# Two-sample cross-attention kernel on one core: all eight parts of the probability-value product in one visit of the z banks, two-bank evacuations, and new orders on every engine

## What is computed

```python
mu, var = mean(input, axis=(1, 2)), var(input, axis=(1, 2))     # per sample
xn = (input - mu) * rsqrt(var + EPS) * gamma + beta
q  = einsum('oc,ncs->nos', Wq, xn) + bq
kv = einsum('od,nds->nos', Wkv, context) + bkv
att = softmax(einsum('nhqc,nhkc->nhqk', q * scale, k * scale), axis=-1)
y   = einsum('nhqk,nhkc->nhqc', att, v)
out = einsum('co,nos->ncs', Wo, y) + bo
return input + out
```

## Time and profile before

| | |
|---|---|
| median of three runs | 808.37 us |
| profiled execution: its time | 807.66 us |
| profiled execution: span | 805.8 us |
| TensorE busy (matmuls) | 686.3 us, 85% of the span |
| TensorE weight loads | 445.8 us, 55% |
| VectorE busy | 678.0 us, 84% |
| ScalarE busy | 621.6 us, 77% |
| GpSimd busy | 581.7 us, 72% |
| DMA queue of SyncE | 21.6% of what 16 DMA engines could do |
| mean granted clock of TensorE | 0.983 of full |

### The profile page before, as it was taken

How to read it: one execution, slowest core, us unless ns; L and a number is a source line. 1 busy time by engine, 2 the same in 40 slices (tenths; PEclk the granted TensorE clock), 3 DMA queues, 4 the chain that set the end, 5 groups by cost and what they waited for, 6 DMA issues and landing times.

```text
span 805.8 us, 29956 instructions
## 1 busy us (share of the span) xinstructions
PE 686.3 (85%) x11204; PEld 445.8 (55%) x11204; DVE 678.0 (84%) x1124; ACT 621.6 (77%) x2248; POOL 581.7 (72%) x360
## 2 busy tenths in 40 slices
PE   5689988889888888988888988888898888898886
PEld 4355655555655555655555655555565555566453
DVE  1589888898988889898889898888989888989883
ACT  2578778787788878687878788878778778878872
POOL 1478677777777878677877777788777687777763
PEclk9989999999999999999999999999999999999998
DMA  5112222222221222222222221221222122222110
GB/s 111 37 48 68 62 57 67 60 62 62 62 63 51 72 52 64 59 62 53 68 59 58 62 64 52 64 72 51 62 62 62 49 72 53 64 65 52 44 40 15
DMA packets 74814, 47.56 MB, mean 59 GB/s; under 512 B 33748, under 2 KB 74708, under 8 KB 74772
## 3 DMA queue, kind: packets, MB, share of 16 engines
q1 hardware_dynamic: 72848, 46.59, 21.6%
q10 hardware_dynamic: 1924, 0.40, 0.3%
HBM read 25.96 MB, written 4.19 MB: 37 GB/s over the span
## 4 chain that ended last, share of the span: by engine, by line
POOL 41%; issue 37%; PE 9%; DVE 9%; ACT 2%; POOLq 1%; DMA 1%; SPq 1%; ACTq 0%; DVEq 0%
POOL probs L639 32%; POOL xhat L654 6%; DVE probs_t L551 4%; PE z L401 4%; DVE neg_max L538 3%; PE fill L367 3%; POOL rstd L649 3%; ACT probs L483 2%; POOLq L101 1%; PE z L379 1%; DMA wv<-in_L_xattn_Wkv 1%; ACT t L492 1%; DVE recip L544 0%; DVE y L594 0%; SPq L234 0%
## 5 line engine op out<-in xcount | busy, mean ns | idle before, releaser
L639 POOL TENSOR_TENSOR probs<-probs,recip 128x1024 f32<-128x1024 f32 x256 | 483.1, 1893 | 188.5 <-DVE recip L544 184.3
L483 ACT ACTIVATE probs<-fill,neg_max 128x256 f32<-128x256 f32 x1024 | 470.5, 483 | 149.9 <-DVE neg_max L538 149.6
L551 DVE STREAM_TRANSPOSE probs_t<-probs 128x1024 f32<-128x1024 f32 x256 | 313.7, 1225 | 49.7 <-POOL probs L639 46.2
L538 DVE TENSOR_REDUCE neg_max<-fill 128x4 f32<-128x1024 f32 x256 | 306.6, 1198 | 36.3 <-PE fill L367 36.0
L401 PE MATMUL z<-probs_t,ctx_keys 32*64 32x256 f32 x8192 | 260.3, 388 | 69.5 <-DVE probs_t L551 68.3
L367 PE MATMUL fill<-c,t 64*128 64x256 f32 x2048 | 285.6, 404 | 17.6 <-ACT probs L483 13.2
L401 PEld LDWEIGHTS z<-probs_t,ctx_keys 32*64 32x64 f32 x8192 | 177.0, 134 | 139.5 <-issue 69.7
L367 PEld LDWEIGHTS fill<-c,t 64*128 64x128 f32 x2048 | 182.8, 189 | 120.0 <-ACT probs L483 58.4
L483 ACT ACTIVATION_READ_ACCUMULATOR probs<-fill,neg_max 128x1 f32 x1024 | 220.1, 215 | 0.0
L492 ACT ACTIVATE t<-z,d_col 128x512 f32<-128x512 f32 x128 | 77.8, 708 | 7.3 <-PE z L379 7.3
L379 PE MATMUL z<-xhat,qk_gamma 64*128 64x512 f32 x256 | 66.5, 637 | 16.2 <-POOL xhat L654 16.2
(11 more groups left out here) (38 smaller groups left out, 91.1 us busy)
## 6 DMA issues: line engine op xcount, KB each, us to landing
ctx_keys<-ctx_turned SPq DMA_DIRECT2D x512, 32.0 KB, 1.8
x<-in_x SPq DMA_DIRECT2D x64, 128.0 KB, 2.8
c<-in_ctx SPq DMA_DIRECT2D x64, 128.0 KB, 2.7
ctx_rows<-in_ctx SPq DMA_DIRECT2D x128, 32.0 KB, 1.8
x_res<-in_x SPq DMA_DIRECT2D x32, 128.0 KB, 2.2
out<-y SPq DMA_DIRECT2D x32, 128.0 KB, 1.8
wq<-in_L_xattn_Wq ACTq DMA_DIRECT2D x2, 128.0 KB
wv<-in_L_xattn_Wkv SPq DMA_DIRECT2D x2, 128.0 KB
```

The lines of the kernel that those rows point to most:

```text
L483: ins = act.activation(probs[:, k % SLOTS, g, :], bank[:, K * qt:K * qt + K], ACT.Exp, bias=neg_max[:, k, g:g + 1], accum_out=denom[:, k, ...
L538: dve.tensor_reduce(neg_max[:, k, :], fill[k % PAIRS_OF_BANKS][:, :, :].rearrange("p o (t k) -> p (o t) k", t=QT), AX.X, ALU.max, negate=T ...
L551: dve.transpose(probs_t[p][:, s, :, :, hp, :, :].rearrange("p b o t j -> p o t b j"), probs[:, k % SLOTS, :, :].rearrange("p (o t) (b j) - ...
L639: pool.tensor_tensor(p, p, recip[:, k, :].unsqueeze(2).broadcast_to([128, 2 * QT, K]), ALU.mult).then_inc(probs_ready, 1)
```

## The change

Both samples of a pair are mixed in one visit of the z banks. All eight parts run first; then come two copies, each of two whole banks for both samples (`copy_z(pair, i)`), then `project_in` of the next pair, whose first half waits for the first copy and whose second half for the second, `query_rows`, `project_out`, and `sum_means`. `normalise` is now one call for each sample, with a place of its own in the order. The five tables are all new. The count of every kind of instruction stays the same.

```diff
-PE_ORDER = (at('scores', 0.00, 0.68, 3.21, 6.25, 7.62, 9.46, 11.81, 12.81)
-            + at('mix', 13.43, 14.12, 14.75, 15.37, 20.94, 21.62, 22.93, 24.31) + at('project_out', 26.33)
+PE_ORDER = (at('scores', 0.00, 1.12, 3.45, 4.98, 7.20, 10.10, 10.87, 13.52)
+            + at('mix', 18.00, 18.76, 20.22, 21.75, 22.51, 23.96, 24.73, 25.42) + at('project_out', 30.21)
...
             def project_in(pair, i):
                 if i == 0:
                     wait(pe, xhat_ready, pair.count(PS, PS))
-                    if pair.shift(-2).exists():
-                        wait(pe, z_ready, pair.shift(-2).count(PS, 1))
+                if pair.shift(-2).exists():
+                    wait(pe, z_ready, pair.shift(-2).count(2, i + 1))
...
                     if pair.shift(-1).exists():
                         wait(pe, y_ready, pair.shift(-1).count(1, 1))
+                    if pair.shift(1).exists():
+                        wait(pe, t_ready, pair.shift(1).count(HP, HP))
                     if pair.shift(2).exists():
                         wait(pe, variance_ready, pair.shift(2).count(1, 1))
                 elif i == MIXES:
                     wait(pe, turned, pair.count(STEPS, STEPS))
-                    wait(pe, z_ready, pair.count(PS, 1))
-                    if pair.shift(2).exists():
-                        wait(pe, t_ready, pair.shift(2).count(HP, HP))
...
             def project_out(pair):
-                wait(pe, z_ready, pair.count(PS, PS))
+                wait(pe, z_ready, pair.count(2, 2))
+                if pair.shift(2).exists():
+                    wait(pe, t_ready, pair.shift(2).count(HP, 1))
...
             def sum_means(pair):
                 wait(pe, mean_var_ready, pair.count(PS, PS))
-                if pair.shift(-3).exists():
-                    wait(pe, z_ready, pair.shift(-3).count(PS, PS))
-                elif pair.shift(-1).exists():
-                    wait(pe, t_ready, pair.shift(-1).count(HP, HP))
+                if pair.shift(-1).exists():
+                    wait(pe, t_ready, pair.shift(-1).count(HP, 2))
...
-            def copy_z(pair, s):
-                wait(act, mixed, pair.count(PS, s + 1))
-                if s == 0 and pair.shift(-1).exists():
+            def copy_z(pair, i):
+                wait(act, mixed, pair.count(PS, PS))
+                if i == 0 and pair.shift(-1).exists():
                     wait(act, summed_out, pair.shift(-1).count(1, 1))
-                act.copy(z_sb[:, s, :, :].rearrange("p h (t a j) -> p a (h t) j", t=QT, a=QB),
-                         z[:, :, S * s:S * s + S].rearrange("p a (g j) -> p a g j", j=32)).then_inc(z_ready, 1)
+                act.copy(z_sb[:, :, :, :].rearrange("p s h (t a j) -> p a (s h t) j", t=QT, a=QB)[:, 2 * i:2 * i + 2, :, :],
+                         z[:, 2 * i:2 * i + 2, :].rearrange("p a (g j) -> p a g j", j=32)).then_inc(z_ready, 1)
...
-            def normalise(pair):
+            def normalise(pair, s):
                 p = pair.parity()
-                for s in range(PS):
-                    pool.tensor_scalar(xhat[:, s, :], x2[p][:, s, :], mean[:, s:s + 1], rstd[:, s:s + 1],
-                                       ALU.subtract, ALU.mult).then_inc(xhat_ready, 1)
+                pool.tensor_scalar(xhat[:, s, :], x2[p][:, s, :], mean[:, s:s + 1], rstd[:, s:s + 1],
+                                   ALU.subtract, ALU.mult).then_inc(xhat_ready, 1)
```

More of the change, by code:

```diff
@@ L37, in at @@
     return [(time, kind, i) for i, time in enumerate(times)]
-PE_ORDER = (at('scores', 0.00, 0.68, 3.21, 6.25, 7.62, 9.46, 11.81, 12.81)
-            + at('mix', 13.43, 14.12, 14.75, 15.37, 20.94, 21.62, 22.93, 24.31) + at('project_out', 26.33)
[L43 to L55, removed]
+PE_ORDER = (at('scores', 0.00, 1.12, 3.45, 4.98, 7.20, 10.10, 10.87, 13.52)
+            + at('mix', 18.00, 18.76, 20.22, 21.75, 22.51, 23.96, 24.73, 25.42) + at('project_out', 30.21)
+            + at('project_in', -4.44, -3.75) + at('mean', -16.22) + at('var', -15.24))
@@ new lines @@
+ACT_ORDER = (at('exp', 1.93, 3.39, 5.57, 7.31, 9.13, 12.04, 13.84, 15.63) + at('t', -2.59, -0.79, 1.00, 1.43)
+             + at('z', 26.50, 27.24))
+DVE_ORDER = (at('weights', -2.64, 0.96) + at('max', 0.98, 2.44, 4.61, 6.36, 8.18, 11.09, 11.92, 14.52)
+             + at('recip', 4.28, 6.30, 8.04, 9.87, 10.78, 13.60, 15.35, 18.38)
+             + at('turn', 7.19, 9.01, 9.93, 12.75, 13.66, 15.41, 19.42, 21.45) + at('moments', -30.11)
+             + at('mean_var', -28.73) + at('spread', -15.74) + at('sample_var', -14.19)
+             + at('turn_context', 4.34) + at('result', 32.64))
@@ L58, in in_order @@
+POOL_ORDER = (at('divide', 5.51, 6.92, 8.33, 10.63, 12.04, 13.80, 15.54, 18.58) + at('root', -12.01)
+              + at('norm', -10.47, -6.26))
+SYNC_ORDER = (at('load_x', -5.06) + at('load_c', 14.52) + at('load_ct', 5.14) + at('spread_context', 4.94)
+              + at('residual', 24.64) + at('store', 33.14))
 def in_order(order):
@@ L665, in steps @@
                     else:
-                        normalise(owner)
+                        normalise(owner, item)
             walk(pool, steps)
```

## The result

| | before | after |
|---|---|---|
| median | 809.12 us (4 runs) | 746.45 us (4 runs, 746.12 to 747.64) |
| ratio, 95% interval | | 0.923 (0.920 to 0.926) |
| span of the profiled execution | 805.8 us | 744.9 us |
| mean granted clock of TensorE | 0.983 | 0.998 |

A forecast was written before the change was run, and what follows sets the result against it. The prediction saw a dependence loop, no saturated engine, bounding the 23.79 us period. A new 21.40 us path saves 31 × 2.39 = 74.1 us: span 805.8 to 731.7, forecast 734 us, range 717 to 768.

The forecast's parts named there:

- The old loop: Dependences through POOL's root and normalisations, the second z-bank visit and DVE; said to set the old 23.79 us period.
- The middle: Span from the first S0 score to the last, 31 periods; forecast to lose 31 × 2.39 = 74.1 us.
- the prices stay, the order moves: Whole kernel: the change adds and removes no instruction, so durations from the old trace were kept.
- its 21.0 as a floor: DVE's busy time per period, 21.0 us; at a 21.4 period it would be 98% busy.
- the path of 21.40: Longest closed path found, round the z banks: PE mixes and scores, DVE maxima, ACT exponentials and t; forecast period 21.40 us.
- my own two criteria: Forecast is wrong if the period exceeds 21.8 us, or if mix M0 waits for something other than t3.
- the walk: Step-by-step pass through the new order tables with old distances, seeking the longest closed path; it summed to 21.40 us.
- The cost of the split is nothing: POOL: giving each sample's normalisation its own place uses the same two instructions, so costs nothing.
- SP: DMA queue with the store moved ahead: path of 20.3 us, hidden by 1.1; rival of x late, slower than before, .04.
- The clock rival: TensorE's granted clock falls once every pass as mix runs shorten: period 22.8, time 777 us; chance .05.
- the irregular rest: The 4.6 us between first and last S0 score beyond 31 regular periods; left unchanged in the forecast.
- The first rival: DVE keeps half its waits for POOL and PE: period 22.35, time 763 us, range 746 to 790; chance .28.

The follow-up runs named there:

- run 6: Changed kernel with its normalisations cut to 2 of 256 columns; 746.66 us, ratio 0.924.
- run 5: Kernel before with its normalisations cut to 2 of 256 columns; 790.18 us, ratio 0.977.
- run 9: Changed kernel with root and both normalisations put back ahead of division D7 on POOL, single z-bank visit kept; 766.70 us, ratio 0.949.
- run 2: Changed kernel with the reciprocal of step 6, and so its division, moved behind the mean and spread chain; 733.46 us, ratio 0.909.
- run 3: Changed kernel with one operand and the result of `squared` in PSUM, division left beside it, one DVE instruction more; 732.84 us, ratio 0.907.
- run 10: Changed kernel with both normalisations together behind division D2 instead of split; 791.59 us, ratio 0.978.
- run 12: Changed kernel with both normalisations together behind division D2 and the reciprocal of step 6 behind the spread chain; 763.05 us, ratio 0.944.
- run 8: Changed kernel with the reciprocal of step 6 behind the spread chain and transpose T5 moved behind the variance; 761.22 us, ratio 0.944.

## Why the prediction was right, and where it failed

- **The old loop opened: right.** DVE waits for POOL .8 us instead of 46.2, POOL's root and normalisations stand aside (run 6), and neither part alone does it: with the normalisations cut short in the kernel before, run 5 gains some 18 us; with the joined visit and all other new orders but POOL's work ahead of D7, run 9 gains some 41; the change gains 62.
- **The size: right in the range, 12 us off in the point.** The middle gave 56.9 us against 74.1; head and tail gave 4.0 that I had left as they were.
- **The step that failed is the price of DVE's stretch.** I took its durations from the rows before ("the prices stay, the order moves") and its 21.0 as a floor at which the path of 21.40 stays free. But `squared` moved from an idle time of POOL into D6 and grew from .16 to .72. That is .56 × 31 = 17 us. Runs 2 and 3 take it away in two ways and come to 733.5 and 732.8, beside a forecast of 734. That they meet it is in part luck: the period of run 2 is 21.52 to 21.56 and not 21.40, some 4 us over 31 periods, and the head and the tail gave about as much back.
- **The closed path was another one.** I had t3 to M0 to S5 to E5 to t3. The trace closes over the maxima of S0, E0, S2, S5 and DVE. M0 waits for the variance and not for t3, and the period is 22.0: by my own two criteria ("over 21.8, or if M0 waits for something other than t3") the mechanism as forecast was wrong. That the number 734 is met once `squared` is short does not prove my path either: 22.00 less .56 is 21.44, mine was 21.40, and the two lie side by side by accident. So even at the prices of the rows before, the walk had missed a loop as long as its own. In run 2 it is again this loop that closes, by the starts of the maxima of S0, E0, S2, S5 (first of two), the maxima of S5 and the next maxima of S0:

```profile
416.19 1.22 DVE L537 TENSOR_REDUCE neg_max<-fill 128x4 f32<-128x1024 f32 x1
...
417.44 0.47 ACT L482 ACTIVATE probs<-fill,neg_max 128x256 f32<-128x256 f32 x1 [0.18 <-DVE neg_max L537]
...
419.54 1.13 PE L366 MATMUL fill<-c,t 64*128 64x256 f32 x8
...
428.46 2.00 PE L366 MATMUL fill<-c,t 64*128 64x256 f32 x16
...
429.65 2.36 DVE L537 TENSOR_REDUCE neg_max<-fill 128x4 f32<-128x1024 f32 x2 [0.21 <-PE fill L366]
...
437.71 1.22 DVE L537 TENSOR_REDUCE neg_max<-fill 128x4 f32<-128x1024 f32 x1
```

The steps are 1.25, 2.10, 8.92, 1.19 and 8.06, together 21.52, and M0 still waits for the variance there (.32 at 417.62).
- **The walk had one price too high.** M3 and M4 took 1.91 (409.15 to 411.06), not 2.10. The 2.78 for M5 to M7 is three quarters of the four parts' duration, 3.71, and not of their distance, 3.64, which gives 2.73; they took 2.77. M4's own wait ended just as its turn came (T7 starts at 408.69, M4's weights load from 409.98) and cost nothing.
- **"The cost of the split is nothing": right but understated.** The split normalisations cost nothing; together they cost 45 us (run 10), or 30 with the short `squared` (run 12). I had named this as free without asking what the alternative costs.
- **SP: right.** The moments wait for DMA three times, at the start, 10.1 us in all. The moved queue costs nothing in the steady part.
- **The clock rival: right to put it low, and the reason was weak.** One double mix of the changed kernel ran slow, at the start (50.10, 2.98 us), and none after it (before 3 of 31), though the runs of mixes are shorter. That took away the three periods longer by 1.4, some 4 us of the irregular rest, which I had left in; the changed kernel has 2.8 of its own there. But in runs 5, 10 and 12 the falls came back with idle times of PE of only 1.2 us ahead of the slow mixes (run 5), or none over 1 us directly ahead (run 10, .36). So "no idle time of 2.42 left" was not a reason. What PE did in common before the falls is not settled: in run 10 PE waited 33.4 us in all before the sums of spreads, and no run tried these waits separately. Idle time alone does not sort the kernels: in run 8 PE waited 57.4 us in all for exponentials, up to 1.09 at a time in the pass shown, at a mean clock of 1.00.
- **The first rival was nearest.** It gave DVE as the limit and 746 to 790 us; 746.45 lies at its edge. Its mechanism, waits of DVE for PE and POOL, was not what happened: these waits, ahead of transposes and maxima, are 16 us in all. DVE was held inside one instruction.

## What to carry to other kernels

A duration read from a trace holds for what ran beside it. When an order moves an instruction of two SBUF tensors next to a long GpSimd instruction, price it with the rest of that instruction's time, and look for a place in an idle time of GpSimd, or read one operand from PSUM. And before one wait is removed, follow every other path that ends at the same time: M0's wait looked like the cause and was worth nothing.

## What the runs showed that was not expected

- A DVE multiply of 128x2 values takes .16 us beside nothing and .72 beside POOL's 1.89 us division, until that ends; with one operand and the result in PSUM .17 beside the same division, and a subtraction with one operand in PSUM and the result in SBUF .14. Reduces and transposes (one SBUF or PSUM input) ran beside divisions in both kernels at 1.2 us.
- A matmul group whose own wait ends as its turn comes goes on at the pace of the group before it (1.91 for two parts with the wait between them, 1.91 without).
- The mean granted clock was .948 in run 10 and .959 in run 5, against .998 in the changed kernel and 1.00 in run 8. A double mix at the lower clock takes up to 3.7 us instead of 1.99, 1.2 against 2.4 GHz, the clock's two levels. In run 10 one pass ran slow and the next at full clock with the same instructions and all but the same wait ahead (.36 and .42), so the row directly ahead does not decide it.
